# Operations moved in the prologue and the first two steps of an attention and feed-forward kernel

## The chip, the cores and the metric

The kernel runs on one core of one Trainium2 chip. The metric is the device time of one execution, in microseconds: 298.79 us is the median of three runs of the kernel before (298.68 to 300.03).

## What is computed

x has the shape (4, 1024, 256), all of it is float32. Two blocks follow each other, each on a layer norm without weights and each with a residual. The first is a causal linear attention (16 query heads, 4 key heads, head size 16), the second a channel mix with a token shift:

```python
a = layernorm(x)
q, k, v = a @ Wq + bq, (a @ Wk + bk) @ Wc @ We, (a @ Wv + bv) @ Wc @ We
qf, kf = elu(q) + 1, elu(k) + 1
num = einsum(qf, cumsum(kf * v));  den = einsum(qf, cumsum(kf)) + 1e-6
y = a + (num / den) @ Wo + bo
x = x + layernorm(y) * gamma + beta
z = layernorm(x);  zp = z moved by one token
r = sigmoid((mu_r * z + (1 - mu_r) * zp) @ W_r.T)
k = relu((mu_k * z + (1 - mu_k) * zp) @ W_k.T) ** 2
out = x + r * (k @ W_v.T)
```

## The kernel before

The 1024 tokens are cut into 8 chunks of 128; a chunk of all 4 batches is one unit of work (tokens on the partitions, 4 x 256 numbers in each). The running sums over tokens are carried from chunk to chunk, so the chunks follow each other. The code is one hand-written program for each engine, and a wait on a counter (semaphore) stands wherever one engine needs another; no planner sets the order. Within an engine and within a DMA queue the order is the order of the code.

A **prologue** prepares the weights and does chunk 0's keys, values and queries. Then come **steps** c = 0 to 6 and a **finale**. A step is a software pipeline of three chunks: scores, outputs and division of chunk c; keys, values, queries and denominators of chunk n = c+1; the output projection and second residual of chunk m = c-1; the channel mix of chunk f = c-2. So steps 0 and 1 have no channel mix (f is below 0), and step 0 no second residual either. Step 2 is the first full one.

**The prologue on each engine.** SyncE issues the loads of x chunk 0, Wk and Wv, bk and bv (`bias_in`), x chunk 1, the three feed-forward weights, the row vectors and Wo (`rows_in`) and x chunk 2. ScalarE issues Wc and We, then Wq and four pieces of bq (`q_in`); then it waits for `q_in` (ahead of L842), copies Wq into another order, copies `wcT` and `wkvT` out of PSUM once TensorE has transposed them (L636), copies `cewe`, copies aT (`a_out(0)`), and copies `wkv_sb` and `bkv_bc`. TensorE fills waits with products of the identity (`keep_busy`, L626), transposes (L632, L636), multiplies Wc and We (L640), forms Wk Wc We and Wv Wc We (L645) and the bias rows (L649), transposes chunk 0's a_tok (L655), and goes on to `keys_values(0)` (L364), `queries` (L370), `keys_transposed` (L376), `state_increments` (L385), `scores` (L419) and `denominators` (L393). VectorE computes chunk 0's statistics (L878 to L884), waits for `q_in`, forms -bq and 1+bq (L1129, L1130), scales chunk 0 into a_tok (`norm_x_scale(0)`, L1136), scales the rows of ones by bk and bv (L1143), computes chunk 1's statistics, and then the keys' and queries' features. GpSimd makes the identity and head masks, chunk 0's rstd (L211 to L221), further constants (`causal`, `head_rows`, zT's zeroes, L321 to L335), chunk 1's rstd, and after `prod` of chunk 0 it adds bo and beta (`add_bo`, L243; `add_beta`, L250).

**A step on TensorE**: `transpose_z` (L456, not in steps 0 and 1), `transpose_a` (L357), `spread_reciprocals` (L402), the output projection (L448) or in step 0 the first feed-forward weight's transposes (L485), `scores(c, 1)`, `keys_values`, mix_r (L470), `outputs(c, 0)` (L435, L440), scores, queries, outputs, keys_transposed, state_increments, scores, mix_k (L463), outputs, mix_v (L478), denominators, outputs, mix_v, `scores(n, 0)`. `outputs(c, b)` needs `divide(c, b-1)` and `mask(c, b)` of VectorE; mix_k needs both queries' features (`s_qf`).

**On VectorE**, steps 0 and 1 run the same function as the others, with parts left out: mask (L953), statistics of the next x, add_residual (L978) with its statistics, mask, keys and values (L900, L901), `centre` (L988: y minus its mean, times gamma), key_features (L905, L908), `second_residual` (L999), divide (L967), mask, queries (L914), divide, states (L929), `second_stats`, key_sums (L923), mask, divide, `reciprocal` (L936, L938), divide. In full steps the token shifts (L1013) and gates (L1026) are added. **On GpSimd**: token_difference (L266), norm_x, first_norm, add_bo, add_beta, then second_norm and `denominator_terms` (L258, prod), in step 1 in the order denominator_terms, second_norm. `add_beta(n)` waits for second_residual of chunk n-2, and the load of x chunk n+3 waits for it in its turn. **On ScalarE**: `a_out(n)`, `reciprocals(c)` (rden_bc), normalise_x, keys, queries, values, state blocks, keys_transposed, normalise_z (L755).

## Time and profile before

| | |
|---|---|
| median of the runs | 298.79 us |
| the profiled execution, its own time | 300.61 us |
| its span | 298.80 us |
| mean granted clock of TensorE | 0.969 |
| TensorE busy | 272.9 us, 91% |
| VectorE busy | 235.1 us, 79% |
| ScalarE busy | 145.4 us, 49% |
| GpSimd busy | 128.8 us, 43% |

The span is the profiler's, from the first to the last instruction; the execution's own time is a little longer. Step 2 begins with the transposes of z at 79.7 us, step 3 31.79 us later. In the timelines neighbouring instructions of a line are merged, and an idle time in brackets says what ended it; in the chain of waits each piece is what the next one had waited for. A granted clock of 1.00 is TensorE's full level, 2.4 GHz; 0.50 is 1.2 GHz.

### The profile page before, as it was taken

How to read it: one execution, taken by the hardware profiler on the slowest of the kernel's cores; microseconds unless marked ns; L12 is line 12 of the kernel's file. 1: busy time of each engine (PE TensorE's matmuls, PEld its weight loads, DVE VectorE, ACT ScalarE, POOL GpSimd, SP SyncE). 2: the span in 40 equal slices, each digit the busy share in tenths (PEclk: the TensorE clock that was granted, in tenths of full speed). 3: DMA queues.
4: the chain of work that ended last, by engine and by line, in shares of the span. 5: the costliest groups of instructions: out<-in, count | busy, mean ns of one | idle time of the engine just before them, and what ended most of it. 6: DMA issues, size and time to landing. Idle time of an engine off the chain costs nothing.

```text
span 298.8 us, 7425 instructions
## 1 busy us (share of the span) xinstructions
PE 272.9 (91%) x2923; PEld 192.7 (65%) x2923; DVE 235.1 (79%) x578; ACT 145.4 (49%) x294; POOL 128.8 (43%) x151
## 2 busy tenths in 40 slices
PE   7598798887899999999999999999999999977894
PEld 7565655745685578756885588557865677654663
DVE  6629569799799959996899779985999558989433
ACT  1238655545454756376455844484247520453540
POOL 2711660244474447436753567354344414063310
PEclk9789799997799999999999999999999999999999
DMA  6900202002000013000400020001100110002012
GB/s 175 274 12 3 72 1 72 2 3 70 3 2 0 2 37 105 2 3 3 140 2 0 2 73 0 2 2 35 37 5 0 37 37 2 0 0 71 35 37 70
DMA packets 12178, 10.73 MB, mean 36 GB/s; under 512 B 2288, under 2 KB 12144, under 8 KB 12144
## 3 DMA queue, kind: packets, MB, share of 16 engines
q1 hardware_dynamic: 11392, 9.97, 10.5%
q8 instruction: 23, 0.38, 0.5%
q10 hardware_dynamic: 752, 0.30, 0.4%
q14 instruction: 11, 0.09, 0.1%
HBM read 6.07 MB, written 4.19 MB: 34 GB/s over the span
## 4 chain that ended last, share of the span: by engine, by line
PE 76%; DVE 10%; ACT 5%; issue 3%; DMA 2%; ACTq 1%; POOL 1%; DVEq 0%
PE ps_x L448 9%; PE ps_x L478 8%; PE ps_x L370 7%; PE ps_x L463 6%; PE ps_z L419 6%; PE ps_x L470 6%; PE ps_y L440 5%; PE ps_x L364 5%; PE ps_y L435 5%; PE ps_z L470 4%; PE ps_x L456 2%; PE ps_z L463 2%; PE ps_x L357 2%; DVE probs L953 2%; PE ps_z L402 2%
## 5 line engine op out<-in xcount | busy, mean ns | idle before, releaser
L953 DVE TENSOR_TENSOR probs<-ps_z,causal 128x512 f32<-128x512 f32 x64 | 40.8, 679 | 6.7 <-PE ps_z L419 6.7
L273 POOL TENSOR_TENSOR out_tok<-tanh_r,x_tok 128x512 f32<-128x512 f32 x14 | 18.7, 1338 | 27.7 <-DVE tanh_r L1026 27.7
L1026 DVE SCALAR_TENSOR_TENSOR tanh_r<-tanh_r,ps_x 128x512 f32<-128x512 f32 x13 | 8.9, 687 | 27.0 <-PE ps_x L478 27.0
L448 PE MATMUL ps_x<-wo_sb,oT 128*128 128x256 f32 x128 | 29.6, 382 | 0.0
L250 POOL TENSOR_TENSOR xb_tok<-x_in,beta_bc 128x1024 f32<-128x1024 f32 x8 | 18.9, 2361 | 24.8 <-DVE x_tok L999 24.8
L370 PE MATMUL ps_x<-aT,wq_sb 128*128 128x512 f32 x60 | 27.8, 604 | 0.0
L478 PE MATMUL ps_x<-wvT,k_act 128*128 128x256 f32 x104 | 25.6, 389 | 1.0 <-ACT k_act L773 1.0
L243 POOL TENSOR_TENSOR abo_tok<-a_tok,bo_bc 128x1024 f32<-128x1024 f32 x8 | 18.9, 2360 | 17.3 <-issue 12.6
L217 POOL TENSOR_TENSOR neg_mean<-mv,neg_one 128x4 f32<-128x4 f32 x16 | 5.0, 311 | 49.4 <-DVE mv L884 49.4
L448 PEld LDWEIGHTS ps_x<-wo_sb,oT 128*128 128x128 f32 x128 | 23.6, 190 | 3.8 <-issue 0.9
L213 POOL TENSOR_TENSOR rstd<-rstd,neg_half 128x4 f32<-128x4 f32 x24 | 24.9, 1037 | 1.9
L419 PE MATMUL ps_z<-qf,kfT 32*128 32x128 f32 x512 | 23.5, 298 | 1.6 <-ACT rden_bc L684 0.7
L988 DVE SCALAR_TENSOR_TENSOR y_tok<-y_tok,mv,gamma_bc 128x256 f32<-128x256 f32 x32 | 23.9, 805 | 0.0
L435 PE MATMUL ps_y<-qf,state 32*32 32x128 f32 x512 | 20.9, 279 | 2.9 <-DVE oT L967 2.9
L419 PEld LDWEIGHTS ps_z<-qf,kfT 32*128 32x128 f32 x512 | 17.5, 187 | 8.7 <-issue 6.7
L435 PEld LDWEIGHTS ps_y<-qf,state 32*32 32x32 f32 x512 | 12.1, 105 | 16.9 <-issue 12.0
L478 PEld LDWEIGHTS ps_x<-wvT,k_act 128*128 128x128 f32 x104 | 18.9, 190 | 5.5 <-ACT k_act L773 2.4
L705 ACT ACTIVATE eq<-ps_x,neg_bq 128x512 f32<-128x512 f32 x15 | 10.3, 687 | 23.2 <-PE ps_x L370 23.2
L440 PE MATMUL ps_y<-probs,v_pad 128*32 128x128 f32 x512 | 21.5, 287 | 0.0
L684 ACT ACTIVATE zT<-ps_x 128x512 f32<-128x512 f32 x16 | 8.7, 595 | 22.6 <-PE ps_x L456 22.4
L266 POOL TENSOR_TENSOR dz<-zT 128x512 f32<-128x512 f32 x14 | 14.3, 1040 | 11.9 <-ACT zT L684 11.9
L463 PE MATMUL ps_x<-xk,wkT 128*128 128x512 f32 x40 | 18.5, 605 | 0.0
(133 smaller groups left out, 584.2 us busy)
## 6 DMA issues: line engine op xcount, KB each, us to landing
x_in<-in_L_attn_x_dram SPq DMA_DIRECT2D x8, 512.0 KB, 4.3
out_dram<-out_tok SPq DMA_DIRECT2D x16, 256.0 KB, 2.1
xr<-in_L_attn_Wq_dram ACTq DMA_DIRECT2D x1, 256.0 KB, 4.0
xk<-in_L_ffn_W_r_dram SPq DMA_DIRECT2D x1, 256.0 KB, 5.4
xk<-in_L_ffn_W_k_dram SPq DMA_DIRECT2D x1, 256.0 KB, 5.7
xr<-in_L_ffn_W_v_dram SPq DMA_DIRECT2D x1, 256.0 KB, 7.2
wo_sb<-in_L_attn_Wo_dram SPq DMA_DIRECT2D x4, 64.0 KB, 4.8
bo_bc<-in_L_attn_bo_dram SPq DMA_DIRECT2D x1, 128.0 KB, 5.5
```

The costliest lines, as they stand in the source:

```text
L213: PL.tensor_tensor(dst[:], dst[:], neg_half[:], ALU.pow).then_inc(done, 1)
L243: PL.tensor_tensor(abo_tok[n % 2][:], a_tok[n % 2][:], bo_bc[:].unsqueeze(1).to_broadcast([P, NB, D]), ALU.add).then_inc(s_ab, 1)
L370: last = mm(bk_[:, :], wq_sb[:, k, a, :], aT[:, k, :], start=(k == 0), stop=(k == KD - 1))
L419: last = mm(ps_z[:, g, u * P:(u + 1) * P], kfT[c % 2][rows, 2 * b + u, :, :], qf[c % 2][rows, :, t0:t0 + HALF], start=True, stop=True, ski ...
L435: mm(ps_y[rows, off + u * P:off + (u + 1) * P], state[rows, slot, b, :, :], qf[c % 2][rows, :, t0:t0 + HALF], start=(u == 0), stop=False, ...
L440: last = mm(ps_y[32 * g:32 * g + 32, off + u * P:off + (u + 1) * P], v_pad[c % 2][:, b, u, g, :, :], probs[b % 2][:, g, u * P:(u + 1) * P] ...
L448: last = mm(bk_[:, (b % 2) * D:(b % 2 + 1) * D], oT[m % 2][:, a, b, :], wo_sb[:, a, :], start=(a == 0), stop=(a == 1))
L463: last = mm(bk_[:, :], wkT[:, k, n * P:(n + 1) * P], xk[:, k, :, :], start=(k == 0), stop=(k == KD - 1))
L470: last = mm(bk_[:, (b % 2) * D:(b % 2 + 1) * D], xr[:, k, b, :], wrT[:, k, :], start=(k == 0), stop=(k == KD - 1))
L478: last = mm(bk_[:, (b % 2) * D:(b % 2 + 1) * D], k_act[:, k, b * P:(b + 1) * P], wvT[:, k, :], start=(k == 0), stop=(k == KD - 1))
L953: V.tensor_tensor(probs[b % 2][:, 2 * h:2 * h + 2, :].rearrange("p g (r s) -> p g r s", s=HALF), ps_z[:, 2 * h:2 * h + 2, 0:2 * P].rearran ...
L988: V.scalar_tensor_tensor(out=y_tok[:, b, :], in0=y_tok[:, b, :], scalar=mv1[:, b, 0:1], in1=gamma_bc[:], op0=ALU.subtract, op1=ALU.mult).t ...
```

## The change

In the prologue ScalarE's wait for `q_in` and its copies of Wq move behind `a_out(0)`, and the copies of wkv_sb and bkv_bc move ahead of it; its wait on `dve_const` is for 2 instead of 1. VectorE scales the bias rows (L1143) ahead of `norm_x_scale(0)`, and its wait for `q_in` with the two operations on bq moves behind `norm_x(1)`. GpSimd waits for chunk 0's four scalings before `causal` and the other constants. One of TensorE's `keep_busy(2)` becomes `keep_busy(1)`.

In every step ScalarE does `reciprocals(c)` between the two copies of aT. In step 0 TensorE does `scores(0, 1)` ahead of the first feed-forward weight's transposes. Steps 0 and 1 get a VectorE function of their own, `short_step`: `centre` goes between the two queries, `second_residual` behind the last mask, `second_stats` behind divide(c, 2), and key_sums ahead of both. On GpSimd `add_bo` and `add_beta` go to the end of steps 0 and 1, in step 1 behind denominator_terms and second_norm.

```diff
--- before.py
+++ after.py
@@ -281,16 +281,19 @@
                     norm_x(n + 1)
                 if m >= 0:
                     first_norm(m)
-                if c == 0:
-                    pool.wait_ge(s_kf, 2 * n + 2)
-                add_bo(n)
-                add_beta(n)
                 if f >= 0:
+                    add_bo(n)
+                    add_beta(n)
                     second_norm(m)
                     denominator_terms(n)
-                elif m >= 0:
-                    denominator_terms(n)
-                    second_norm(m)
+                else:
+                    if m >= 0:
+                        denominator_terms(n)
+                        second_norm(m)
+                    else:
+                        pool.wait_ge(s_kf, 2 * n + 2)
+                    add_bo(n)
+                    add_beta(n)
                 if f >= 0:
                     finish(f)
 
@@ -318,6 +321,7 @@
             PL.memset(neg_half[:], -0.5).then_inc(pool_const, 1)
             pool.wait_ge(pool_const, 1)
             norm_x(0)
+            pool.wait_ge(s_a, 4)
             link(PL.memset(causal[:], 1.0))
             for u in range(2):
                 half = causal[HALF * u:HALF * u + HALF, :]
@@ -504,11 +508,11 @@
                     out_projection(m, 0, x1)
                     pe.wait_ge(s_aT, 2 * n + 1)
                     out_projection(m, 1, x2)
-                else:
+                scores(c, 1)
+                if m < 0:
                     pe.wait_ge(ffn_w_in, FFN_IN)
                     pe.wait_ge(s_qf, 2)
                     ffn_weight(0, x1)
-                scores(c, 1)
                 keys_values(n)
                 if f >= 0:
                     pe.wait_ge(s_y, 2 * m + 1)
@@ -638,7 +642,7 @@
             keep_busy(2)
             pe.wait_ge(prep_sb, 1)
             mm(z0[0:64, 128:128 + KV], wcT[0:64, :], we_in[0:64, :], start=True, stop=True).then_inc(prep_ps, 1)
-            keep_busy(2)
+            keep_busy(1)
             pe.wait_ge(prep_sb, 2)
             for i in range(2):
                 for k in range(KD):
@@ -683,12 +687,11 @@
             def copy(dst, src, **kw):
                 return AC.activation(dst, src, ACT.Copy, **kw)
 
-            def a_out(n):
+            def a_out(n, k):
                 if n >= 1:
                     act.wait_ge(s_q_ps, 2 * n)
-                for k, bk_ in ((0, x2), (1, x0)):
-                    act.wait_ge(s_aT_ps, 2 * n + k + 1)
-                    copy(aT[:, k, :], bk_[:, :]).then_inc(s_aT, 1)
+                act.wait_ge(s_aT_ps, 2 * n + k + 1)
+                copy(aT[:, k, :], (x2, x0)[k][:, :]).then_inc(s_aT, 1)
 
             def keys(n):
                 act.wait_ge(s_kv, 2 * n + 1)
@@ -782,8 +785,9 @@
                 n, m, f = c + 1, c - 1, c - 2
                 if f >= 0:
                     shift_z(f, x0, x1)
-                a_out(n)
+                a_out(n, 0)
                 reciprocals(c)
+                a_out(n, 1)
                 if c == 0:
                     act.wait_ge(ffn_w_ps, 1)
                     copy(flat(wrT), x1[:, :]).then_inc(ffn_w_sb, 1)
@@ -839,21 +843,22 @@
                     act.dma_start(dst, src).then_inc(c_in, 16)
                 for dst, src in q_loads:
                     act.dma_start(dst, src).then_inc(q_in, 16)
+            act.wait_ge(prep_ps, 1)
+            copy(wcT[0:64, :], z0[0:64, 0:64])
+            copy(wkvT[0:64, :, :].rearrange("p i n -> p (i n)"), z1[0:64, :]).then_inc(prep_sb, 1)
+            act.wait_ge(prep_ps, 2)
+            copy(cewe[0:64, :], z0[0:64, 128:128 + KV]).then_inc(prep_sb, 1)
+            act.wait_ge(prep_ps, 3)
+            copy(flat(wkv_sb), ps_y[:, 0:256])
+            copy(bkv_bc[:], ps_y[:, 256:384]).then_inc(prep_sb, 1)
+            a_out(0, 0)
+            a_out(0, 1)
             act.wait_ge(q_in, Q_IN)
             for k in range(KD):
                 last = copy(wq_sb[:, k, :, :].rearrange("p a (g m) -> p a g m", g=G),
                             wq_in[:, k, :].rearrange("p (g a m) -> p a g m", g=G, a=2))
             last.then_inc(wq_ready, 1)
-            act.wait_ge(prep_ps, 1)
-            copy(wcT[0:64, :], z0[0:64, 0:64])
-            copy(wkvT[0:64, :, :].rearrange("p i n -> p (i n)"), z1[0:64, :]).then_inc(prep_sb, 1)
-            act.wait_ge(prep_ps, 2)
-            copy(cewe[0:64, :], z0[0:64, 128:128 + KV]).then_inc(prep_sb, 1)
-            a_out(0)
-            act.wait_ge(prep_ps, 3)
-            copy(flat(wkv_sb), ps_y[:, 0:256])
-            copy(bkv_bc[:], ps_y[:, 256:384]).then_inc(prep_sb, 1)
-            act.wait_ge(dve_const, 1)
+            act.wait_ge(dve_const, 2)
             keys(0)
             queries(0, 0, x1)
             act.wait_ge(s_kT_ps, 1)
@@ -1033,45 +1038,61 @@
                     reciprocal(0)
                 if n + 1 < NC:
                     norm_x(n + 1)
-                if f >= 0:
-                    token_shift(f, 0, *for_r)
-                    token_shift(f, 1, *for_r)
+                if f < 0:
+                    short_step(c, n, m)
+                    return
+                token_shift(f, 0, *for_r)
+                token_shift(f, 1, *for_r)
+                add_residual(m, 0, x1)
+                add_residual(m, 1, x2)
+                mask(c, 1)
+                keys_values(n)
+                centre(m)
+                key_features(n)
+                second_residual(m)
+                divide(c, 0)
+                mask(c, 2)
+                queries(n, 0, x0)
+                token_shift(f, 0, *for_k)
+                token_shift(f, 1, *for_k)
+                queries(n, 1, x1)
+                divide(c, 1)
+                states(n)
+                second_stats(m)
+                key_sums(n)
+                mask(c, 3)
+                divide(c, 2)
+                gate(f, 0, x1)
+                reciprocal(n)
+                divide(c, 3)
+                gate(f, 1, x2)
+
+            def short_step(c, n, m):
                 if m >= 0:
                     add_residual(m, 0, x1)
                     add_residual(m, 1, x2)
                 mask(c, 1)
                 keys_values(n)
-                if m >= 0:
-                    centre(m)
                 key_features(n)
-                if m >= 0:
-                    second_residual(m)
                 divide(c, 0)
                 mask(c, 2)
                 queries(n, 0, x0)
-                if f >= 0:
-                    token_shift(f, 0, *for_k)
-                    token_shift(f, 1, *for_k)
+                if m >= 0:
+                    centre(m)
                 queries(n, 1, x1)
                 divide(c, 1)
                 states(n)
-                if f >= 0:
+                key_sums(n)
+                if m < 0:
+                    denominator_terms(n)
+                mask(c, 3)
+                if m >= 0:
+                    second_residual(m)
+                divide(c, 2)
+                if m >= 0:
                     second_stats(m)
-                    key_sums(n)
-                else:
-                    key_sums(n)
-                    if m < 0:
-                        denominator_terms(n)
-                    else:
-                        second_stats(m)
-                mask(c, 3)
-                divide(c, 2)
-                if f >= 0:
-                    gate(f, 0, x1)
                 reciprocal(n)
                 divide(c, 3)
-                if f >= 0:
-                    gate(f, 1, x2)
 
             def finale(c):
                 m, f = c - 1, c - 2
@@ -1125,9 +1146,11 @@
             dve.wait_ge(pool_const, 1)
             for j in range(2):
                 V.tensor_reduce(row_mask[:, j:j + 1], head_cols[:, 0, j:8:2], AX_X, ALU.add)
-            dve.wait_ge(q_in, Q_IN)
-            V.tensor_scalar(neg_bq[:], bq_col[:], -1.0, None, ALU.mult)
-            V.tensor_scalar(bq_1[:], bq_col[:], 1.0, None, ALU.add).then_inc(dve_const, 1)
+            dve.wait_ge(bias_in, BIAS_IN)
+            dve.wait_ge(dve_const, 1)
+            for i in range(2):
+                last = V.tensor_scalar(bkv_lhs[0:64, i, :], ones[0:64, :], bkv_col[0:64, i:i + 1], None, ALU.mult)
+            last.then_inc(bias_lhs, 1)
 
             def norm_x_scale(n):
                 dve.wait_ge(s_st0, 8 * n + 8)
@@ -1137,12 +1160,10 @@
                                     ALU.mult).then_inc(s_a, 1)
 
             norm_x_scale(0)
-            dve.wait_ge(bias_in, BIAS_IN)
-            dve.wait_ge(dve_const, 2)
-            for i in range(2):
-                last = V.tensor_scalar(bkv_lhs[0:64, i, :], ones[0:64, :], bkv_col[0:64, i:i + 1], None, ALU.mult)
-            last.then_inc(bias_lhs, 1)
             norm_x(1)
+            dve.wait_ge(q_in, Q_IN)
+            V.tensor_scalar(neg_bq[:], bq_col[:], -1.0, None, ALU.mult)
+            V.tensor_scalar(bq_1[:], bq_col[:], 1.0, None, ALU.add).then_inc(dve_const, 1)
             dve.wait_ge(prep_sb, 3)
             keys_values(0)
             key_features(0)
```

## Rows read from the trace of the kernel before

**Rows 1.** The page, parts 1 and 2: busy time, granted clock in slices of 7.47 us.

```profile
PE 272.9 (91%) x2923; PEld 192.7 (65%) x2923; DVE 235.1 (79%) x578; ACT 145.4 (49%) x294; POOL 128.8 (43%) x151
...
PEclk9789799997799999999999999999999999999999
```

**Rows 2.** The chain of waits, prologue: start us, us, what.

```profile
10.64 0.47 PE ps_z L640 x2
...
12.27 1.90 PE ps_y L645 x8
14.16 0.85 PE ps_y L649 x4
15.02 1.70 PE ps_x L655 x7
...
17.82 0.28 ACT wkv_sb L684
...
18.32 2.07 PE ps_x L364 x16
```

**Rows 3.** Three stretches by engine, granted clock last but two.

```profile
7.00:10.40 3.40, 0.62 (x5) 0.43 (x3) 1.12 (x4) 1.12 (x4) 2.85 (x9) 1.00 1.02 339
10.60:17.20 6.60, 6.56 (x29) 6.10 (x30) 3.47 (x13) 0.68 (x2) 3.98 (x8) 0.50 0.62 163
...
31.10:34.40 3.30, 3.00 (x24) 2.37 (x24) 1.39 (x9) 1.12 (x2) 3.22 (x4) 0.50 0.03 3
```

**Rows 4.** Timelines of ScalarE, VectorE and GpSimd, prologue: start us, us, what, idle before.

```profile
9.28 0.72 ACT L684 ACTIVATE wq_sb<-xr 128x256 f32<-128x256 f32 x2 [3.25 <-DMA bq_col<-in_L_attn_bq_dram]
...
9.43 2.36 DVE L1136 TENSOR_SCALAR a_tok<-x_in,mv,rstd 128x256 f32<-128x256 f32 x4
...
22.46 1.38 DVE L1136 TENSOR_SCALAR a_tok<-x_in,mv,rstd 128x256 f32<-128x256 f32 x4
...
7.33 1.02 POOL L213 TENSOR_TENSOR rstd<-rstd,neg_half 128x4 f32<-128x4 f32 x1
...
12.40 0.96 POOL L335 MEMSET zT<- 128x1032 f32 x1
```

**Rows 5.** The chain of waits, step 0.

```profile
31.00 1.19 PE ps_z L402 x16
...
33.88 0.92 ACT rden_bc L684
...
35.57 1.98 PE ps_x L364 x16
```

**Rows 6.** Step 1: timelines of VectorE, TensorE, GpSimd, line L988's durations, the chain.

```profile
61.81 3.42 DVE L988 SCALAR_TENSOR_TENSOR y_tok<-y_tok,mv,gamma_bc 128x256 f32<-128x256 f32 x4
...
66.14 1.67 DVE L999 SCALAR_TENSOR_TENSOR x_tok<-y_tok,rstd,xb_tok 128x256 f32<-128x256 f32 x4
...
68.20 0.70 PE L435 MATMUL ps_y<-qf,state 32*32 32x128 f32 x16 [2.01 <-DVE oT L967]
...
73.48 2.34 POOL L258 TENSOR_TENSOR prod<-qf,ksum 128x1024 f32<-128x1024 f32 x1 [3.23 <-DVE ksum L923]
...
L988 DVE SCALAR_TENSOR_TENSOR y_tok<-y_tok,mv,gamma_bc x4: 472/472/2227, 61.8 to 64.8; 128x256 f32<-128x256 f32 x4
...
79.70 1.02 PE ps_x L456 x8
```

**Rows 7.** Step 2: timelines of GpSimd and VectorE, the chain.

```profile
81.39 2.04 POOL L266 TENSOR_TENSOR dz<-zT 128x512 f32<-128x512 f32 x2 [3.88 <-ACT zT L684]
83.39 0.65 POOL L217 TENSOR_TENSOR neg_mean<-mv,neg_one 128x4 f32<-128x4 f32 x1
...
82.74 1.90 DVE L1013 SCALAR_TENSOR_TENSOR xr<-dz,mu_r_col,zT 128x512 f32<-128x512 f32 x2
...
99.19 0.74 DVE L914 SCALAR_TENSOR_TENSOR qf<-ps_x,bq,eq 128x512 f32<-128x512 f32 x1
...
100.22 3.65 PE ps_x L463 x8
```

## The prediction

> **What bounds the kernel now.** I read the page first. TensorE is busy for 91% of the span, and the granted clock is at nine tenths or more in every slice from the twelfth (82 us) to the end, while five of the eleven slices before are lower: the time that can be saved lies ahead of about 82 us [rows 1]. From there on the chain of waits is one unbroken line of TensorE work, and nothing in the loops of steps 2 to 6 or in the finale is touched by the diff. So the question is when step 2 starts, and whether it starts in good order.
>
> The chain over the prologue comes next [rows 2]. What precedes its first row is not TensorE: ScalarE sat idle for 3.25 us until the last bq load landed, then copied wq, and only then copied wcT and wkvT, which TensorE needed at 10.64 [rows 4]. From there to 16.72 TensorE works through L640 to L655, all of it at a granted clock of 0.50, so 1.2 GHz, after it had stood idle from 7.6 to 10.6, while the level was still 1.00 [rows 2, 3]. Then ScalarE copies aT, and after that wkv and bkv_bc, and chunk 0's keys and values begin at 18.32.
>
> In step 0 the chain passes aT's second half, then rden_bc, then scores(0,1) [rows 5]. In step 1 TensorE stands idle for 2.01 us (up to 68.20) until divide(1,0), which sits behind centre and second_residual on VectorE, and again before the denominators, which wait for GpSimd's prod [rows 6].
>
> **The change, part by part.** Every sum is in the times of the profiled execution, whose span is 298.80 us; its own time of 300.61 us is 1.82 us over the median of the runs, 298.79. I take the saving off the median.
>
> *ScalarE's prologue order.* The copies of wcT and wkvT no longer stand behind the bq wait. TensorE's transposes for them end at about 7.0 and ScalarE's table load at 6.0, so the copies run about 7.05 to 7.7 where they ran 10.00 to 10.60: L640 starts at 7.7 instead of 10.64, 2.95 us earlier. The cost of the moved wq copy (0.72 us) lies under keys_values(0), which takes 2.07 us; it would show only if that cover were shorter.
>
> *The level of the clock.* The idle stretch that preceded the low level shrinks from 3 us to some tenths, so I take the full level for L640 to L655. L640 and the copy of cewe take 0.8 us before L645 can start (one keep_busy fits in it, the second would have pushed; taking it out costs nothing). L645's 8 and L649's 4 products took 1.90 and 0.85 us at the low level. At the full one I take the pace of L364, 2.07/16 = 0.13 us each, so 1.0 and 0.5; for the 8 transposes L456's 1.02 us [rows 2, 6]. They end at 7.7 + 0.8 + 1.0 + 0.5 + 1.0 = 11.0 instead of 16.72. At the low level throughout it would be 7.7 + 0.8 + 1.90 + 0.85 + 1.70 = 12.95: these are the two bounds, 5.7 and 3.8 us saved. I take 5.7, since the nearest row, the stretch up to 10.4, has the full level [rows 3].
>
> *VectorE's side.* a_tok has to be there. It waited for the bq constants until 9.43, then took 2.36 us beside GpSimd's constants; the same four operations alone took 1.38 [rows 4]. New: GpSimd's rstd ends at 8.35 as before, a_tok runs 8.4 to 9.8, and the last transposes want it after 10.5. The bias scaling (0.71 us) moves ahead of it; the load it waits for, issued at 2.90, landed at 7.0, so it runs 7.0 to 7.7 beside GpSimd's rstd. How far it holds GpSimd up no row says; a tiny GpSimd operation beside VectorE's token shift took 0.65 instead of 0.20 [rows 7]. Two such delays are 0.9 us at most and zero at least; I take 0.2, and even 0.7 is still hidden by TensorE. The Trainium skill ("SBUF — State Buffer", Who interferes with whom) says that tensor_scalar can take the port pair shared with GpSimd for a whole instruction and block it; by that rule this reordering puts a blocker ahead of a_tok, and the sum would lose the part beyond 0.7 us, nothing or a few tenths.
>
> *wkv and bkv_bc before aT.* They go into the time of the transposes: the 0.50 us between 17.82 and 18.32 leave the chain [rows 2]. Prologue: 5.7 + 0.5 = 6.2, and I keep 6.1 for the gaps between engines. Keys and values of chunk 0 then start at 12.2.
>
> *GpSimd's constants* wait for a_tok: 9.8 plus the 4.8 us that they took (8.6 to 13.36 [rows 4]) is 14.6, and behind them chunk 1's rstd, 1.5 us, is ready at 16.1. VectorE asks for it after key_features(0), at 22.46 - 6.1 = 16.4. Hidden by 0.3 us; if the constants took longer, each tenth beyond that would pass into a_tok(1). Bounds 0 and 0.5; I take 0. TensorE and VectorE wait for the loads of rows before step 0; they were issued by 10.7 and have landed by 15.7, while the new step 0 starts at 22.5: no cost. bq's constants now follow norm_x(1), about 12.4, before ScalarE's first wait for them at 14.8: none.
>
> *Step 0.* spread_reciprocals ends at 32.2; rden_bc no longer follows the second aT copy, so it runs to 33.25, beside the transposes, and scores(0,1) starts there rather than at 34.84. The transposed FFN weight, taken out of its front, follows, at the mixed clock of this stretch (0.7 to 1.06 us). keys_values(1) starts at 34.95 instead of 35.57: 0.6 us [rows 5]. Between 0.3 and 0.8.
>
> *Step 1, in the time of before.* centre goes behind queries(2,0), second_residual behind mask(1,3), GpSimd's abo and xb behind second_norm. divide(1,0) is then done at 63.5 and TensorE does not idle at 66.2. VectorE: qf at 66.6; centre alone, 1.67 us as its sister L999, to 68.2 (it had 3.42 because its first operation, 2227 ns against 472, stood out GpSimd's abo); second qf 68.9; divide 69.2; tail 69.45; key sums to 71.0. prod then runs 71.05 to 73.4, 2.4 us earlier than before. But VectorE reaches second_residual at 72.2, while prod runs: by the same row its first operation stands it out, so it ends at 74.95, divide(1,2) at 75.3, second_stats at 77.05, where it was 75.11. GpSimd's second_norm gives nbias at 78.8 (was 77.5), z_tok is complete at 80.9, and the transposes of z end at about 81.05 against 80.72 [rows 6]. **TensorE's gain in step 1 is thus gone again at its end: 0.35 us later, not earlier.**
>
> *Step 2.* abo and xb, 2.36 each, now run from 78.8 to 83.4. Behind them on GpSimd queue the token differences, which ran 81.39 to 83.43 and will run 83.4 to 85.45, and norm_x(4). VectorE's token shifts wait for them and end at 86.45 instead of 84.6: VectorE is 1.87 us late. It had no idle time from there to the second qf at 99.93, for which TensorE's mix_k at 100.22 waits [rows 7]. The cover is 0.29 us, so mix_k is late by **1.6 us** (the 0.35 is inside it). Later VectorE idles 1.8 us before the first gate, so this is paid once. The fifth load of x, behind xb on SP's queue, leaves 13 us later and is wanted at about 112: none. Bounds: 0 and 2.5.
>
> Sum: 6.1 + 0.6 - 1.6 = 5.1 us, **293.7 us**.
>
> **The rivals.**
> (a) *Steps 1 and 2 give nothing back.* If second_residual is not held up by prod, second_stats ends 1.1 us earlier, and the delay at mix_k shrinks to about 0.5; if TensorE also keeps the full level in step 0, where it ran at 0.50 from 31.1 to 34.4 [rows 3], another 1 us goes. 291.2 to 292.6, say 292.0. For it: there is less work in front; against: the 2227 ns row. Chance 0.20.
> (b) *The prologue's chain stays at the low level*: 1.9 us less saved, 295.6 us. For it: there are still small gaps; against: the level was full up to 10.4 [rows 3]. The Trainium skill ("TensorE: Matmul & The Clock Gate", Part 1) says that the array's default is the throttled state, released by sustained work. The profile shows 1.00 from the first microsecond, so by that rule the chain would be slow, and by the row it isn't. Chance 0.16.
> (c) *No change*: the gain is caught by something that does not move. To leave less than 1.5 us it would have to become ready at about 27, not 22.5; the loads are there by 15.7. Or (b) together with a second fall of the clock in step 2. Chance 0.06.
> (d) *Slower: GpSimd's lag is carried on.* If the late token differences came back in each of steps 2 to 6, mix_k would wait 1.6 to 1.7 us five times, 8.3 us, and 298.8 - 6.7 + 8.3 = 300.4. It decides from four steps on. Against it: VectorE idles 1.8 and 1.5 us before the gates of step 2 and GpSimd 1.7 and 2.4 us, and from step 2 the order on GpSimd is the old one. Chance 0.04.
>
> **How the numbers follow.** The forecast has 0.54. Its own bounds are 292.5 to 294.8. The range takes in (a) and (b) with its bounds: 291.2 to 296.0. An effect under 0.5%, 1.5 us, can't be told from none. Faster by more: forecast, (a) and (b), 0.90; within it 0.06; slower 0.04.
>
> **What would show it.** keys_values(0) (L364) starts near 12.2, with the clock at 1.00 from 7 to 17; step 0's keys_values near 28.3; in step 1 no idle time before the second outputs; the first L999 of step 1 far over 1000 ns and prod ahead of it; token differences of step 2 starting about 2 us later against TensorE, and a wait of some 1.3 us before the first mix_k. Steps 3 to 6 keep their 31.79 us. The prediction is wrong if L364 starts later than 14, or if step 2 takes longer than 34 us or not longer at all.

## The result and the profile after

The changed kernel took 295.57 us in the median of four runs (294.52 to 296.34), the kernel before 298.74 in four (298.08 to 300.03): a ratio of 0.9886, interval 0.9838 to 0.9934, so 3.2 us faster. Measured again later, in the same rounds as the kernel before (300.66), it took 295.27: 0.9811, interval 0.9780 to 0.9843, 5.4 us. 5.1 had been forecast. The forecast of 293.7 us took that off the median of 298.79; the measured 295.57 lies in its range (291.2 to 296.0), but outside the forecast's own bounds of 292.5 to 294.8. The profiled execution has a span of 293.3 us, 5.5 less than that of before. That is more than the 3.2 us between the medians, because before's profiled execution (300.61) lay 1.9 us over its median, and the changed kernel's (295.08) 0.5 us under its own.

The page, against [rows 1]: GpSimd, VectorE and ScalarE did the same work, and the granted clock is low in only two slices ahead of step 3 where it was in five. A further low stretch came late, at 264.7 to 268.1 us.

```profile
PE 270.1 (92%) x2921; PEld 189.6 (65%) x2921; DVE 233.7 (80%) x578; ACT 145.4 (50%) x294; POOL 129.0 (44%) x151
...
PEclk9999999995799999999999999999999999997999
```

The prologue, timelines of TensorE, ScalarE, VectorE and GpSimd (start us, us, what, idle time before), against [rows 2, 4]:

```profile
7.53 0.33 PE L644 MATMUL ps_z<-we_in,wcT 64*64 64x64 f32 x2 [0.34 <-ACT k_act L688]
...
8.21 1.10 PE L649 MATMUL ps_y<-cewe,k_act 64*128 64x64 f32 x8
9.15 0.61 PE L653 MATMUL ps_y<-cewe,k_act 64*128 64x64 f32 x4
9.68 1.09 PE L659 MATMUL ps_x<-ident,a_tok 128*128 128x128 f32 x8
...
11.93 2.02 PE L368 MATMUL ps_x<-wkv_sb,aT 128*128 128x128 f32 x16 [0.49 <-ACT aT L688]
...
9.79 0.39 ACT L688 ACTIVATE wkv_sb<-ps_y 128x256 f32<-128x256 f32 x1 [1.68 <-PE ps_y L653]
...
8.74 1.38 DVE L1159 TENSOR_SCALAR a_tok<-x_in,mv,rstd 128x256 f32<-128x256 f32 x4 [0.61 <-POOL rstd L213]
...
16.79 1.38 DVE L1159 TENSOR_SCALAR a_tok<-x_in,mv,rstd 128x256 f32<-128x256 f32 x4 [0.65 <-POOL rstd L213]
...
7.66 0.47 DVE L1152 TENSOR_SCALAR k_act<-ones,bkv_col 64x128 f32<-64x128 f32 x2 [0.53 <-DMA bkv_col<-in_L_attn_bv_dram]
...
7.61 1.02 POOL L213 TENSOR_TENSOR rstd<-rstd,neg_half 128x4 f32<-128x4 f32 x1
...
15.48 1.20 POOL L213 TENSOR_TENSOR rstd<-rstd,neg_half 128x4 f32<-128x4 f32 x1
```

Everything of before's 10.64 to 16.72 now stands between 7.53 and 10.8, because the engine came earlier and because it ran at the full level: the products on cewe (now L649) took 1.10 us instead of 1.90. wkv_sb is copied before aT, not after it. keys_values of chunk 0 starts at 11.93, 6.39 us earlier. The second a_tok row shows the one thing that got worse: chunk 1's scaling waited 0.65 us for GpSimd's rstd.

Three stretches by engine (granted clock last but two), against [rows 3]:

```profile
10.60:17.20 6.60, 5.58 (x34) 3.88 (x33) 3.61 (x17) 3.87 (x9) 5.36 (x12) 1.00 0.70 183
31.10:34.40 3.30, 3.30 (x19) 1.52 (x12) 2.55 (x6) 1.28 (x3) 2.17 (x1) 1.00 0.00 0
66.80:76.50 9.70, 8.29 (x81) 6.08 (x82) 6.59 (x26) 4.72 (x9) 7.37 (x8) 0.50 0.01 3
```

From L644 on the low level is gone from the prologue, and in this execution from step 0 too; it came back behind step 1's waits, from 66.7 to 76.9, for 10.2 us. Steps 1 and 2, VectorE, GpSimd and TensorE, against [rows 6, 7]:

```profile
58.58 1.66 DVE L993 SCALAR_TENSOR_TENSOR y_tok<-y_tok,mv,gamma_bc 128x256 f32<-128x256 f32 x4
...
64.03 2.81 DVE L1004 SCALAR_TENSOR_TENSOR x_tok<-y_tok,rstd,xb_tok 128x256 f32<-128x256 f32 x4
...
76.34 2.18 DVE L1018 SCALAR_TENSOR_TENSOR xr<-dz,mu_r_col,zT 128x512 f32<-128x512 f32 x2 [2.74 <-POOL dz L266]
...
63.02 2.35 POOL L258 TENSOR_TENSOR prod<-qf,ksum 128x1024 f32<-128x1024 f32 x1 [9.58 <-DVE ksum L928]
...
70.64 2.36 POOL L243 TENSOR_TENSOR abo_tok<-a_tok,bo_bc 128x1024 f32<-128x1024 f32 x1
72.96 2.35 POOL L250 TENSOR_TENSOR xb_tok<-x_in,beta_bc 128x1024 f32<-128x1024 f32 x1
75.27 2.04 POOL L266 TENSOR_TENSOR dz<-zT 128x512 f32<-128x512 f32 x2
...
71.47 2.08 PE L460 MATMUL ps_x<-ident,z_tok 128*128 128x128 f32 x8 [0.99 <-ACT z_tok L758]
...
94.52 3.70 PE L467 MATMUL ps_x<-xk,wkT 128*128 128x512 f32 x8
```

centre now takes 1.66 us instead of 3.42. second_residual takes 2.81 instead of 1.67, since prod runs until 65.37; of its four operations one took 1618 ns:

```profile
L1004 DVE SCALAR_TENSOR_TENSOR x_tok<-y_tok,rstd,xb_tok x4: 473/473/1618, 64.0 to 66.4; 128x256 f32<-128x256 f32 x4
```

The token differences (dz) stand behind xb, and VectorE idles 2.74 us for them. keys_values of step 1 started at 50.72, 7.99 us earlier than before, but mix_k at 94.52 is only 5.63 earlier: **2.4 us were given back between the two.** From mix_k to the end it takes 198.8 us (293.3 - 94.5), before 198.65.

### The profile page after: what moved, and what is told of

The parts are those of the page before. It is cut to its first block, busy times and chain, and to the rows that moved or that the text cites. A ratio compares the mean times of both kernels' runs of the same rounds, so it can differ in the third digit from the quotient of the medians.

```text
span 293.3 us, 7428 instructions
## 1 busy us (share of the span) xinstructions
PE 270.1 (92%) x2921; PEld 189.6 (65%) x2921; DVE 233.7 (80%) x578; ACT 145.4 (50%) x294; POOL 129.0 (44%) x151
## 4 chain that ended last, share of the span: by engine, by line
PE 76%; DVE 11%; ACT 5%; POOL 3%; issue 3%; DMA 1%; POOLq 0%; DVEq 0%; ACTq 0%
PE ps_x L452 10%; PE ps_x L374 8%; PE ps_x L482 8%; PE ps_z L423 6%; PE ps_x L467 6%; PE ps_x L474 6%; PE ps_x L368 5%; PE ps_y L444 4%; PE ps_y L439 4%; PE ps_z L467 4%; PE ps_z L474 4%; PE ps_x L460 3%; PE ps_x L361 2%; DVE probs L958 2%; PE ps_z L406 2%
## 5 line engine op out<-in xcount | busy, mean ns | idle before, releaser
L250 POOL TENSOR_TENSOR xb_tok<-x_in,beta_bc 128x1024 f32<-128x1024 f32 x8 | 18.9, 2361 | 20.7 <-DVE x_tok L1004 20.7
L993 DVE SCALAR_TENSOR_TENSOR y_tok<-y_tok,mv,gamma_bc 128x256 f32<-128x256 f32 x32 | 22.1, 750 | 0.0
L758 ACT ACTIVATE z_tok<-x_tok,nbias,rstd 128x256 f32<-128x256 f32 x32 | 16.5, 591 | 7.2 <-POOL nbias L221 7.2
```

The source lines that it names most:

```text
L993: V.scalar_tensor_tensor(out=y_tok[:, b, :], in0=y_tok[:, b, :], scalar=mv1[:, b, 0:1], in1=gamma_bc[:], op0=ALU.subtract, op1=ALU.mult).t ...
```

## The experiments

All were timed in five rounds, in three groups, each beside the kernel before (medians 300.13, 300.31 and 300.66 us); a ratio is to before in the same rounds. The table has the starts of chunk 0's keys_values (K0), step 1's keys_values (K1) and the first mix_k (M) in each profile, their distance, and where the clock's records have it at 0.50 ahead of M. From M to the end each needs 198.6 to 198.9 us, so M tells the span; the two longest of these, changed and e_keep_bo_early, have 3.4 us at the low level from about 265 us on.

| kernel | K0 | K1 | M | M - K1 | clock at 0.50 | ratio to before, interval |
|---|---|---|---|---|---|---|
| before | 18.32 | 58.71 | 100.15 | 41.4 | 10.6-17.5, 31.1-34.5, 68.7-72.1, 75.5-78.9 | |
| b_again | 18.55 | 58.59 | 100.71 | 42.1 | 9.6-19.8, 74.4-81.3 | 1.0029, 0.9994-1.0063 |
| e_act_only | 16.71 | 56.77 | 98.93 | 42.2 | 11.3-18.1, 72.7-79.5 | 0.9936, 0.9911-0.9961 |
| e_prologue | 12.73 | 52.56 | 94.60 | 42.0 | 10.2-13.6, 68.2-75.1 | 0.9815, 0.9762-0.9868 |
| e_steps | 18.17 | 59.21 | 102.58 | 43.4 | 9.5-19.7, 33.4-36.8, 74.3-84.6 | 1.0143, 1.0100-1.0186 |
| changed | 11.93 | 50.72 | 94.52 | 43.8 | 66.7-76.9 | 0.9886, 0.9838-0.9934 |
| a_again | 11.92 | 50.68 | 93.77 | 43.1 | 66.9-70.3 | 0.9811, 0.9780-0.9843 |
| e_no_poolwait | 12.93 | 52.02 | 95.12 | 43.1 | 10.2-13.6, 68.2-71.7 | 0.9819, 0.9790-0.9849 |
| e_keepclock | 12.22 | 50.98 | 94.08 | 43.1 | none | 0.9865, 0.9817-0.9913 |
| e_keep_bo_early | 11.79 | 52.12 | 94.32 | 42.2 | 26.3-29.7 | 0.9819, 0.9787-0.9851 |
| e_step1_old | 11.80 | 52.12 | 92.18 | 40.1 | 26.3-29.7 | 0.9732, 0.9701-0.9763 |
| e_dve_old | 11.90 | 50.67 | 90.15 | 39.5 | 66.9-70.3 | 0.9690, 0.9662-0.9717 |
| e_dve_old_beta | 11.63 | 50.42 | 89.99 | 39.6 | 66.8-70.2 | 0.9716, 0.9685-0.9747 |
| e_best | 12.72 | 51.85 | 90.34 | 38.5 | 10.1-13.5 | 0.9640, 0.9610-0.9670 |

**The kernel before again** (b_again; no edit).

> The kernel before, unchanged, timed against itself and profiled a second time. Its profile was 1.8 us over the median of its runs, and the two profiles differ by 5.5 us in span while the medians differ by 3.2. Theory A (what the clock does between stages differs from run to run): another profile shows the low level of the clock at other places than 10.6 to 17.2, 31.1 to 34.4 and 68 to 79 us, above all not in step 0, and a span of 296.5 to 298; keys_values of step 0 (L364) then starts 1 us or so earlier, near 34.5. Theory B (the profile was a fair sample): the low stretches stand where they stood, span 298.5 to 299.

Its span was 299.4. The low level stood at other places, and step 0 was free of it, as theory A had it, but what that saved was spent by a longer low stretch in the prologue; step 0's keys_values came at 35.39, not near 34.5, and the span that A gave was wrong. The single runs of this program show how far that goes: spans of 295.9 to 296.5 us at a mean granted clock of 0.985 or 0.986, 298.3 to 299.5 at 0.969 to 0.972. So a difference of 1 or 2 us between two profiles of this program says nothing until the low stretches are compared.

**The prologue's edits alone** (e_prologue), and **the steps' edits alone** (e_steps), each on the kernel before.

> The kernel before with only the edits of the prologue (ScalarE's order, VectorE's bias operations, GpSimd's wait, one keep_busy fewer); steps as before. Theory A (the prologue brings 6 us, and the new order of steps 0 and 1 gives back more in step 1 than it brings in step 0): chunk 0's keys_values starts near 12, and with step 1 in its old order all of it arrives, so this kernel is faster than the changed one, 292.5 to 294.5 us, or a ratio near 0.98. Rival B (the prologue's gain is what is lost later, whatever the order of step 1): no faster than the changed kernel, 295.5 or more.

> The kernel before with only the edits of the steps (short_step, GpSimd's order in steps 0 and 1, scores ahead of the weight's transposes, rden_bc between the copies of aT); prologue as before. Theory A: 0.6 us won in step 0 and 1.6 to 2.4 lost from step 1 to step 2, so slower than before by 1 to 2 us, 299.7 to 300.8. Rival B: the steps' edits are worth something, 297 to 298.5.

The prologue's edits alone do as well as the whole change (0.9815 against 0.9811 to 0.9886), and the steps' alone make the kernel slower by 1.4% (303.31 against 300.13 us), more than the 1 to 2 us expected; M - K1 is 43.4, with 10.2 us at the low level in it, and another low stretch stood in step 0. So the gain is the prologue's, and the steps' edits give back more than they bring. How much shows where the clock hardly fell: the two fastest executions of e_prologue had spans of 289.8 and 289.9 us at a mean granted clock of 0.997, the changed kernel 292.2 and 292.4 at 0.994 (a_again), and with TensorE kept busy 292.3 at 1.000 (e_keepclock, the next one). At nearly the full level the steps' edits thus cost about 2.4 us.

**TensorE kept busy in step 1** (e_keepclock).

```diff
+            def hold_clock(count):
+                for _ in range(count):
+                    mm(x1[:, 0:P], ident[:], ident[:], start=True, stop=True)
...
+                if f == 0:
+                    hold_clock(4)
                 if f >= 0:
                     pe.wait_ge(s_rden, c + 1)
...
+                if m == 0:
+                    hold_clock(10)
                 denominators(n)
+                if m == 0:
+                    hold_clock(4)
                 outputs(c, 3)
```

> The changed kernel with products of the identity in step 1's three waits on TensorE (10 pairs ahead of the denominators, 4 behind them, 4 ahead of step 2's transposes of z), so that it does not idle there. In the changed kernel's trace the clock fell to 0.5 between 67 and 77 us and TensorE reached mix_k 2.4 us later than its lead of 8.0 us at step 1 would have given. Theory C (the low level is what costs): clock at 1.00 through that stretch, mix_k about 2 us earlier, 293.5 us or less. Theory A (GpSimd's late token differences and VectorE behind them cost the same by themselves, and the low clock only covers it): the output projection of step 2 runs at full speed, but mix_k then waits 1 to 1.5 us for the second query's features, and no more than 0.7 us is won, 294.9 to 295.6.

Theory A holds, though the median of 294.48 us is 0.4 under its range (theory C wanted 293.5 or less). The clock stayed at 1.00, out_projection of step 2 started 1.35 us earlier (75.06 instead of 76.41), and mix_k only 0.44, since it now waited for the second query's features:

```profile
75.06 3.62 PE L452 MATMUL ps_x<-wo_sb,oT 128*128 128x256 f32 x16
...
94.08 3.70 PE L467 MATMUL ps_x<-xk,wkT 128*128 128x512 f32 x8 [0.92 <-DVE qf L929]
```

The changed kernel's second profile (a_again), with only 3.4 us at the low level, shows the same wait, and M - K1 is the same 43.1:

```profile
93.77 2.41 PE L467 MATMUL ps_x<-xk,wkT 128*128 128x512 f32 x5 [0.93 <-DVE qf L919]
```

> The changed kernel, unchanged, on the chip and in the rounds of the next three. Its runs so far spread over 1.8 us. Expected: a ratio of 0.985 to 0.990 to the kernel before, single runs from 294 to 296.5, and in the profile the wait for second_residual and the late token differences as in its first one. If only the clock decided (rival), the runs would fall apart by 3 us or more as those of the kernel before do.

The ratio came out lower than expected, 0.9811, beside a slower before (300.66); the single runs, 293.96 to 295.98, spread over 2.0 us and not over 3.

So 3.4 us at the low level in step 1 cost nothing here, VectorE's lateness covers them; the other 6.8 in the first profile cost 0.7.

**add_bo(2) ahead of prod** (e_keep_bo_early): as e_keepclock, and in GpSimd's step:

```diff
                     if m >= 0:
+                        add_bo(n)
                         denominator_terms(n)
                         second_norm(m)
                     else:
                         pool.wait_ge(s_kf, 2 * n + 2)
+                        add_bo(n)
-                    add_bo(n)
                     add_beta(n)
```

> The changed kernel with the clock held up by products of the identity as in e_keepclock, and add_bo(2) moved into GpSimd's idle time ahead of prod in step 1. Theory A (mix_k waited 0.92 us for VectorE, which waited for late token differences): the token differences start right behind zT, 1.3 us earlier, the wait ahead of mix_k goes, and mix_k comes at 93.0 to 93.3 instead of 94.08. Rival (mix_k's wait has another origin, such as centre beside add_bo(3)): it stays at 94.

M stands at 94.32, but this execution had the low level in step 0 and entered step 1 1.14 us later; M - K1 fell by 0.9, to 42.2, and mix_k's wait was gone. The late token differences are thus a cost of their own. add_bo had its price too: VectorE's ek, one operation that takes 0.29 us elsewhere, began 0.65 us behind it and stood out the rest of it, until 57.3.

```profile
55.46 1.86 DVE L921 TENSOR_SCALAR ek<-ek 128x256 f32<-128x256 f32 x1
...
54.81 2.36 POOL L243 TENSOR_TENSOR abo_tok<-a_tok,bo_bc 128x1024 f32<-128x1024 f32 x1
```

**Step 1 back in its old order**: on both engines (e_step1_old), on VectorE alone (e_dve_old), and so with add_beta(2) behind step 2's norm_x(4) (e_dve_old_beta). On VectorE:

```diff
                 keys_values(n)
+                if m >= 0:
+                    centre(m)
                 key_features(n)
+                if m >= 0:
+                    second_residual(m)
                 divide(c, 0)
...
-                if m >= 0:
-                    centre(m)
                 queries(n, 1, x1)
...
                 if m < 0:
                     denominator_terms(n)
+                else:
+                    second_stats(m)
                 mask(c, 3)
-                if m >= 0:
-                    second_residual(m)
                 divide(c, 2)
-                if m >= 0:
-                    second_stats(m)
```

and on GpSimd, in e_step1_old only, add_bo(n) and add_beta(n) ahead of denominator_terms(n) again.

> The changed kernel with step 1 in its old order, on VectorE and on GpSimd; the prologue, step 0 and ScalarE's and TensorE's orders stay changed. Theory A (the new order of step 1 gives back what it and the clock in step 0 brought): step 1's keys_values start where the changed kernel has them, 50.7 us, and from there to the first mix_k (L467) it takes 41.5 us as before, not 43.8; mix_k at 92.2, span near 291. Rival B (step 1's order doesn't matter, what is lost is lost by TensorE's clock in whichever order): mix_k at 94 or later, span 293.

> The changed kernel with only VectorE's step 1 in its old order (centre, key_features, second_residual, divide); GpSimd keeps the new one, so no add_bo stands beside centre and nothing stands ahead of prod. Theory A1 (VectorE's order is the worse half, because second_residual now meets prod and second_stats ends late; GpSimd's order by itself is a gain of the 1.7 us that centre waited for it, less about 1.1 us for late token differences): centre 1.7 us instead of 3.4, the transposes of z end near 70, mix_k near 90.3, span near 289. Rival A2 (GpSimd's order is what costs): the token differences start late as in the changed kernel and mix_k stands at 93.5 or later.

> As the one before, and GpSimd's add_beta(2) moved on into step 2, behind norm_x(4). By theory A1 the token differences then wait for zT alone and mix_k comes up to 1 us earlier, 89.3 to 90; but add_beta(2) now stands ahead of first_norm(1), which may take 0.6 us of it back. If late token differences cost nothing (rival), mix_k stands where the run before has it.

e_step1_old starts mix_k at 92.18, where theory A had put it (92.2), though not by the sum it gave: it lost 1.4 us up to K1, with a low stretch in step 0, and its M - K1 is 40.1, not 41.5, because step 1 ran at the full level. e_dve_old gives 90.15 for 90.3. It has both good halves: no add_bo beside centre, and no prod beside second_residual.

```profile
53.77 1.67 DVE L993 SCALAR_TENSOR_TENSOR y_tok<-y_tok,mv,gamma_bc 128x256 f32<-128x256 f32 x4
...
56.35 1.67 DVE L1004 SCALAR_TENSOR_TENSOR x_tok<-y_tok,rstd,xb_tok 128x256 f32<-128x256 f32 x4
...
90.15 3.70 PE L467 MATMUL ps_x<-xk,wkT 128*128 128x512 f32 x8
```

So VectorE's new order of step 1 is what costs, 3.6 us of M - K1 (43.1 in a_again to 39.5, both with the same 3.4 us at the low level); GpSimd's new order, beside VectorE's old one, is a small gain (40.1 to 39.5, and that against a low stretch of 3.4 us). Moving add_beta(2) on changed nothing that can be told: measured from K1 the token differences came 0.4 us earlier, but the next add_bo 0.1 later, and centre of step 2 took 3.83 us beside it instead of 3.42.

**The best version** (e_best): e_dve_old_beta with hold_clock as above in two places.

```diff
+                if c == 0:
+                    hold_clock(4)
                 pe.wait_ge(s_pr, 8 * c + 2)
                 spread_reciprocals(c, (z0, z1, z2, z3))
...
+                if m == 0:
+                    hold_clock(10)
                 denominators(n)
```

> The changed kernel with step 1's VectorE operations in their old order, add_beta(2) behind step 2's norm_x(4), and products of the identity in two of TensorE's waits: 4 pairs ahead of step 0's spread_reciprocals, 10 ahead of step 1's denominators. Theory A with the clock as a second cost: no low level of the clock in steps 0 to 2, the transposes of z end 1.1 us earlier than in e_dve_old_beta, mix_k near 89.1, a ratio near 0.967 and single runs within 1 us of each other. Rival (the clock's fall is always covered by VectorE): as e_dve_old, 0.969, no earlier mix_k.

No low level in steps 0 to 2, and M - K1 is 38.5, the shortest; but this execution had one in the prologue (10.1 to 13.5, where e_best edits nothing) and entered step 1 1.2 us late, so M is 90.34 and not 89.1. The single runs spread over 1.5 us, not within 1. 290.26 us is 3.6% under before and 1.7% under the changed kernel's 295.27. Against e_dve_old (290.52, in other rounds) the intervals overlap: the plain undoing of VectorE's order has nearly all of it.

**Parts of the prologue.** e_act_only has ScalarE's new order and keep_busy(1) alone, on the kernel before; e_no_poolwait is the changed kernel without this line:

```diff
             norm_x(0)
-            pool.wait_ge(s_a, 4)
             link(PL.memset(causal[:], 1.0))
```

> The kernel before with ScalarE's new prologue order and one keep_busy fewer alone; VectorE's and GpSimd's prologue and all steps as before. Theory A (the parts hold each other up: a_tok and the bias rows still wait for bq and run beside GpSimd's constants): L640 starts near 7.6, TensorE then waits until the bias rows are there at 12.4, and chunk 0's keys_values start at 15.1 (full level) to 16.2 (low level), 2.1 to 3.2 us earlier than before, half of the prologue's gain. Rival (ScalarE's order was the whole of it): 12.5.

> The changed kernel without GpSimd's wait for chunk 0's scaling: its constants run beside a_tok again. Theory A (the wait buys a_tok 1 us and costs chunk 1's rstd 1 us, so it is nearly worth nothing): a_tok takes 2.3 instead of 1.4 us, chunk 0's keys_values start 0.7 to 1.0 us later, 12.7, but chunk 1's a_tok no longer waits 0.65 us for rstd, and step 1 starts within 0.3 us of the changed kernel's. Rival (the wait is worth what a_tok gains): all later times are 0.7 to 1.0 later.

ScalarE's order alone moves L640 as much, to 7.38, but TensorE then stands 3.47 us before the bias rows, which VectorE still scales behind bq and a_tok, and its clock falls at 11.3, while it stands:

```profile
12.62 1.11 PE L649 MATMUL ps_y<-cewe,k_act 64*128 64x64 f32 x4 [3.47 <-DVE k_act L1143]
```

K0 is at 16.71, later than either level had given in my sum. The bias rows came 0.2 us later than I had taken; where the other 0.3 went was not looked into. The low level lasted until 18.1, so keys_values took 2.67 us instead of 2.05. The two reorderings are worth 1.6 us with ScalarE's alone and 6.4 with both; VectorE's alone was not run.

The wait on GpSimd is worth nothing that can be measured (0.9819 against 0.9811). Theory A's reason was half wrong: without it a_tok took 1.46 us, not 2.3.

```profile
8.71 1.46 DVE L1158 TENSOR_SCALAR a_tok<-x_in,mv,rstd 128x256 f32<-128x256 f32 x4 [1.09 <-POOL rstd L213]
...
10.16 2.44 POOL L332 TENSOR_SCALAR_AFFINE_SELECT head_rows<-head_rows 32x256 f32<-32x256 f32 x4
```

What had made it 2.36 before was head_rows alone, and a_tok, no longer behind bq, is done when head_rows begins. Its K0 of 12.93, and K1 of 52.02 where at most 51.0 was expected, come of a chain that started 0.34 us later (L643 at 7.87) and of a low stretch from 10.2 on. e_best and e_prologue, which have GpSimd's wait, had that stretch as well. Chunk 1's a_tok no longer waited for rstd, as theory A had it.

## Why the prediction was right

The mechanisms stood as forecast: the prologue brings the gain, step 0 a little, and steps 1 and 2 give some of it back. That the number fits is luck in part. In the two first profiles the terms were 6.4 for 6.1, 1.6 for 0.6 and -2.4 for -1.6, in sum 5.6 for 5.1. At the full level, by the comparisons below, the steps' edits are worth 0.7 and -3.0, so 1.5 of the 5.6 us come of where the low stretches stood in the two executions. The median of 295.57 us is the figure of rival (b), but no profile of the changed kernel shows that rival's cause.

*ScalarE's order and the level of the clock.* L644 (the old L640) at 7.53 for 7.7, the last transposes done at 10.77 for 11.0, K0 at 11.93 for 12.2. Rival (b), a chain at the low level, did not come about, but a short stretch of it from 10.1 or 10.2 to 13.6 is in three of the ten profiles with this prologue (e_no_poolwait counted), and K0 is 0.8 to 1.0 us later there. e_act_only shows what the full level up to there needed: not ScalarE's order by itself, but the bias rows being there before TensorE asked.

One argument against (b) was a misreading: the level is not at 1.00 from the first microsecond. The profile has no record of the clock ahead of its first rise, which comes at 7.2 us in before and at 5.3 in the changed kernel, and a stretch without a record reads as 1.00. The products of the identity tell the level, here in before:

```profile
1.58 4.21 PE L626 MATMUL ps_z<-ident 128*128 128x128 f32 x18 [1.58 <-POOL ident L309]
...
11.05 1.22 PE L626 MATMUL ps_z<-ident 128*128 128x128 f32 x4
...
25.29 1.60 PE L626 MATMUL ps_z<-ident 128*128 128x128 f32 x12
```

From 1.96 us on one starts every 0.21 us, as in the stretch at 0.50 (11.05), and not every 0.11 us as at 1.00 (25.29). So the kernel starts at the low level, and the rule that (b) quotes agrees with the trace. (b) failed because the level had risen before L644, not because it had been full from the start. The rise differs between executions: it came at 5.3 to 5.8 us in six of the ten profiles, at 6.7 to 6.8 in the three with the low stretch from 10.1 on, and at 7.7 in e_keepclock, which had none. Why is not shown.

*VectorE's side.* a_tok took 1.38 us as forecast. The bias scaling beside GpSimd's rstd delayed it by nothing that shows: rstd took 1.02 us in both, though the bias scaling ran beside it (7.66 to 8.13). The Trainium skill's rule of the shared port pair ("SBUF — State Buffer", Who interferes with whom) had put up to some tenths on this, and the trace has none of them; where two SBUF operands or a tensor_scalar met a long GpSimd operation (second_residual 1618 ns, ek 1.86 us), it holds.

*GpSimd's constants.* 4.74 us (10.18 to 14.92) for 4.8, and rstd at 16.68 instead of 16.1, since it began later and took 1.20: a_tok(1) waited 0.65 us, where I had taken 0 of 0 to 0.5. This term was undersized.

*Step 0.* K0 to K1 took 38.8 us in the changed kernel's profiles, and 40.4 before. The edit has about 0.7 of the 1.6 us: e_prologue, with step 0 in its old order, takes 39.8, and e_best and e_no_poolwait, with the new order and the same low stretch around K0, take 39.1. The rest is the low stretch at 31.1 to 34.5 that did not come again, which I had only in rival (a). In e_step1_old and e_keep_bo_early, which have the changed kernel's step 0, one stands at 26.3 to 29.7 and K0 to K1 takes 40.3. I had treated the clock of before's profile as part of the kernel; it is partly the execution's.

*Steps 1 and 2.* This was the argument's core, and it held in its order and, against before's profile, in its size. second_residual was held up by prod, second_stats ended late, the token differences stood behind xb, and mix_k waited for the second query's features, 0.92 and 0.93 us where TensorE was not late itself. M - K1 was forecast at 41.4 + 1.6 = 43.0 and measured at 43.1 (a_again), 43.1 (e_keepclock) and, with 10.2 us at the low level, 43.8. Two things in it were missed. In the first profile there was no wait before mix_k: TensorE came late by its clock, which the text had not foreseen. And before's own 41.4 contained about 1.4 us of low clock: at the full level its order needs 40.1 (e_step1_old), so the new one costs 3 us, not 1.6. Most of that is there at step 1's end already: the last transposes of z end 22.6 us behind K1 in a_again and e_keepclock, 22.0 in before and 20.7 in e_step1_old. I had "0.35 us later"; the measured 0.5 against before is against a step with two low stretches in it.

The prediction's own sign of being wrong, a step 2 of more than 34 us, was met in the first profile: from the transposes of z at 71.47 to those of step 3 at 105.79 it is 34.32 us. It is 33.62 in a_again and 33.63 in e_keepclock, where no low level stands in step 2, against 33.0 by the prediction's terms (31.79 + 1.6 - 0.35). The transposes of z, which wait for z_tok piece by piece and take 1.8 us instead of 1.1, were left out. The text also said that the diff touches nothing in the loops of steps 2 to 6, but ScalarE's reciprocals stand between the two copies of aT in every step now. The steps from 3 on keep their 31.79 us with it.

*The rivals.* (a) did not hold in steps 1 and 2; its part on step 0's clock did, in some executions. Rival (c) is out, by the gain. Against (d): mix_k's wait came once, and M to the end took the same time in every kernel, within 0.3 us.

## What to carry to other kernels

When an operation is moved off one wait, look up what GpSimd will run beside it at the new place: here centre gained 1.8 us by getting away from add_bo, second_residual lost 1.1 by meeting prod, and everything behind it was late. Follow the queue of the engine that got the work (GpSimd's abo and xb ahead of the token differences) into the next stage before calling a stage faster. Compare stage lengths, not spans, and note the clock's low stretches beside each, or an accident of one execution passes for the worth of an edit.

## What the runs showed of the hardware

The same program's low stretches of TensorE's clock (1.2 GHz) come at different places from one execution to the next: 31.1 to 34.5 in one profile of the kernel before and not in the other. In the rounds of b_again one run of this program had a span of 295.9 us at a mean granted clock of 0.986, another 300.7 at 0.966. Every one of the 14 profiles starts at the low level by the pace of its products of the identity, and rises between 4.4 and 7.7 us; its records of the clock begin only there.

A long GpSimd operation held up single VectorE operations of three kinds. A scalar_tensor_tensor on SBUF operands (1618 ns beside prod, 2227 beside add_bo, instead of 472) and a tensor_scalar of 256 numbers (1.86 us instead of 0.29) ended only after it had; three of a_tok's four scalings took 0.72 us instead of 0.41 beside head_rows' selects. Operations with PSUM among their operands were not held up: mask(1,3) took 1.27 us beside prod (1.25 to 1.29 elsewhere), the queries' features 0.75 us beside add_beta (0.74 elsewhere), and a scan 0.46 us beside GpSimd's rstd as without it. centre meets add_bo in each of steps 2 to 6, in both kernels, and its first operation takes 2.2 us there each time.
